# Expert weights of a graph-plus-MoE layer converted as 12 whole chunks through a ring of three, in place of 24 halves through a ring of six

## The reference, cut to what matters

```
x = x + gnn(_layernorm(x), edges, ...)               # two GAT layers, residual products
x = x + ffn(_layernorm(x)[None], ...)[0]
# in ffn, after attention (x is now the sum so far, h2 its layernorm):
gate_logits = h2 @ Wg                                # 625 x 8, top 1, softmax of one = 1
hid = relu(einsum('nd,edf->enf', h2, W1) + b1)       # W1: 8 x 768 x 3072
y   = einsum('enf,efd->end', hid, W2) + b2           # W2: 8 x 3072 x 768
moe = einsum('ne,end->nd', combine, y)
```

## Time and profile before

| | us |
|---|---|
| median of 3 runs (lowest, highest) | 1209.26 (1204.29, 1209.5) |
| the profiled execution | 1207.77 |
| its span in the profile | 1205.9 |
| TensorE matmul busy | 1054.9 (87%) |
| DVE busy | 762.9 (63%) |
| ACT busy | 557.0 (46%) |
| GpSimd busy | 155.0 (13%) |

### The profile page before, as it was taken

One profiled execution on the slowest core, in us unless ns is written; L12 is line 12 of the kernel. 1 busy time (PEld: TensorE's weight loads), 2 busy tenths in 40 slices (PEclk: granted clock), 3 DMA queues, 4 the chain that ended last, 5 costly groups with the idle time before them and its releaser, 6 DMA issues.

```text
span 1205.9 us, 19078 instructions
## 1 busy us (share of the span) xinstructions
PE 1054.9 (87%) x6178; PEld 659.4 (55%) x6179; DVE 762.9 (63%) x1337; ACT 557.0 (46%) x740; POOL 155.0 (13%) x135
## 2 busy tenths in 40 slices
PE   5989778999789769989989307999999999999997
PEld 3555467646656546556768203555555555555554
DVE  6677678773445763449966419893113999889711
ACT  2676556303131234248843018772113777778511
POOL 3100000280003322126001320000000000000000
PEclk9999889999889879989999658999999999999999
DMA  8920200022401440020000389996001999999501
GB/s 310 366 71 0 105 1 1 1 105 77 79 1 65 79 79 1 1 101 2 2 2 1 81 185 390 357 388 230 13 26 32 372 378 391 367 392 374 193 13 29
DMA packets 98378, 170.63 MB, mean 141 GB/s; under 512 B 38611, under 2 KB 38691, under 8 KB 98330
## 3 DMA queue, kind: packets, MB, share of 16 engines
q1 hardware_dynamic: 88138, 145.33, 35.0%
q0 software_dynamic: 6016, 16.80, 4.4%
q10 hardware_dynamic: 4176, 7.87, 2.0%
HBM read 153.19 MB, written 18.79 MB: 143 GB/s over the span
## 4 chain that ended last, share of the span: by engine, by line
PE 67%; DVE 16%; DMA 5%; issue 5%; ACT 4%; POOL 1%; DVEq 1%; ACTq 0%; SPq 0%; POOLq 0%
PE psum L1309 30%; PE psum L1529 15%; PE psum L1508 14%; DMA low<-in_L_ffn_W_dram 2%; DVE area L1250 2%; PE psum L1346 2%; PE psum L1298 2%; DMA sorted_tokens<-area,smalls 2%; PE psum L1517 2%; DVE smalls L900 1%; ACT area L829 1%; PE psum L1425 1%; DVE low L912 1%; DVE area L1156 1%; DMA low<-sorted_tokens 1%
## 5 line engine op out<-in xcount | busy, mean ns | idle before, releaser
L1309 PE MATMUL psum<-area,low 128*125 128x256 f16 (+2 forms) x1080 | 249.1, 392 | 21.6 <-DVE low L1095 11.2
L1250 DVE TENSOR_TENSOR area<-low,area 128x1536 f16<-128x1536 f32 x144 | 245.5, 1753 | 18.3 <-ACT area L829 18.1
L1529 PE MATMUL psum<-area,low 128*128 128x384 f16 x1296 | 217.9, 326 | 5.6 <-DVE area L1250 4.5
L829 ACT ACTIVATE area<-low 128x1536 f16<-128x1536 f32 x144 | 208.2, 1482 | 28.3 <-DMA low<-in_L_ffn_W_dram 20.9
L1508 PE MATMUL psum<-area,low 128*128 128x512 f16 x972 | 220.7, 381 | 0.0
L1309 PEld LDWEIGHTS psum<-area,low 128*125 128x125 f16 (+1 forms) x1080 | 150.8, 151 | 115.0 <-issue 63.4
L1529 PEld LDWEIGHTS psum<-area,low 128*128 128x128 f16 x1296 | 126.4, 98 | 85.3 <-DVE area L1250 6.8
L1309 PE MATMUL psum<-area 125*128 125x64 f16 (+9 forms) x1076 | 145.2, 287 | 16.3 <-DVE area L1237 8.0
L1508 PEld LDWEIGHTS psum<-area,low 128*128 128x128 f16 x972 | 95.5, 98 | 113.8 <-issue 3.0
L1309 PEld LDWEIGHTS psum<-area 125*128 125x128 f16 (+3 forms) x1076 | 93.8, 127 | 51.3 <-issue 14.4
L840 ACT ACTIVATE low<-psum 128x512 f32<-128x512 f32 x54 | 31.9, 591 | 156.5 <-PE psum L1508 143.7
(11 more groups left out here) (203 smaller groups left out, 1253.0 us busy)
## 6 DMA issues: line engine op xcount, KB each, us to landing
low<-in_L_ffn_W_dram SPq DMA_DIRECT2D x144, 768.0 KB, 8.1
area<-in_L_gnn_W_dram SPq DMA_DIRECT2D x2, 3072.0 KB, 11.6
area<-in_L_gnn_Wr_dram SPq DMA_DIRECT2D x2, 3072.0 KB, 15.7
sorted_tokens<-area POOLq DMA_DIRECT2D x3, 1792.0 KB, 16.5
sorted_totals<-area POOLq DMA_DIRECT2D x3, 1792.0 KB, 28.7
low<-sorted_tokens ACTq DMA_DIRECT2D x11, 384.0 KB, 6.9
low<-sorted_totals ACTq DMA_DIRECT2D x9, 384.0 KB, 3.0
area<-in_L_ffn_Wv_dram SPq DMA_DIRECT2D x6, 384.0 KB, 6.3
```

What stands on the lines that cost most here:

```text
L829: act.activation(unit_parts(u)[0], raw_view(u), ACT.Copy).then_inc(high_ok, 1)
L1250: dve.tensor_tensor(low_, raw_view(u), high_, ALU.subtract).then_inc(low_ok, 1)
L1309: ins = pe.matmul(place(name)[0:parts, at:at + w], left(q), right(q)[:, at:at + w], start=(q == 0), stop=(q == k - 1))
L1529: ins = pe.matmul(psum[:, (4 + q) * BANK:(4 + q) * BANK + D // 2], hidT[c % 2][x_][:, j, :], w2_s[c][w_][:, j, q * D // 2:(q + 1) * D // 2 ...
```

## The change

The unit becomes the whole chunk. There are 12 units in place of 24, the ring has 3 places of 3072 columns in place of 6 of 1536 (the same memory in the same order), each unit is one transfer, one ACT operation and one DVE operation. Since 12 units don't divide evenly over 8 slices, STEPS gives the slices 2, 1, 2, 1, 2, 1, 2, 1 units: in halves 4, 2, 4, 2, ... where 3, 3, 3, 3, ... stood. SP's wait for the scattered totals stays ahead of the third chunk.

```diff
-        RING = 6
-        raw = [low[:, at + q * W1W:at + (q + 1) * W1W] for at in (TW, TW + 2 * XW, TW + XW) for q in range(2)]
+        RING = 3
+        raw = [low[:, at:at + 2 * W1W] for at in (TW, TW + 2 * XW, TW + XW)]
...
-        UNITS = [(w, c, q) for s in range(1, C + 2) for w, c in ((1, s - 1), (2, s - 2)) if 0 <= c < C
-                 for q in range(2)]
+        UNITS = [(w, c) for s in range(1, C + 2) for w, c in ((1, s - 1), (2, s - 2)) if 0 <= c < C]
...
-            w, c, q = UNITS[u]
-            n = (KD if w == 1 else CK) // 2
-            return [part[:, q * n:(q + 1) * n, :] for part in (w1_s if w == 1 else w2_s)[c]]
+            w, c = UNITS[u]
+            return (w1_s if w == 1 else w2_s)[c]
...
-            wait_split(eng, a, unit_of[w, c, 1])
+            wait_split(eng, a, unit_of[w, c])
...
-        AHEAD, PER_STEP = 3, U // (C + 2)
-        assert U % (C + 2) == 0
+        AHEAD = 3
+        STEPS = [(0, 2), (2, 3), (3, 5), (5, 6), (6, 8), (8, 9), (9, 11), (11, 12)]
+        assert U == STEPS[-1][1] and len(STEPS) == C + 2
...
-            for u in range(k * PER_STEP, (k + 1) * PER_STEP):
+            for u in range(*STEPS[k]):
                 convert(a, b, u)
...
-                    for u, (w, c, q) in enumerate(UNITS):
-                        if u == 4:
+                    for u, (w, c) in enumerate(UNITS):
+                        if u == 2:
                             sp.wait_ge(totals_scattered, 16 * T)
...
-                            half_chunk = W1[bass.ds(e, 1), q * D // 2:(q + 1) * D // 2, c * CW:(c + 1) * CW]
+                            chunk = W1[bass.ds(e, 1), :, c * CW:(c + 1) * CW]
                         else:
-                            half_chunk = W2[bass.ds(e, 1), c * CW + q * CW // 2:c * CW + (q + 1) * CW // 2, :]
-                        sp.dma_start(raw_view(u), half_chunk.rearrange("a (k p) n -> p (a k) n", p=128))\
+                            chunk = W2[bass.ds(e, 1), c * CW:(c + 1) * CW, :]
+                        sp.dma_start(raw_view(u), chunk.rearrange("a (k p) n -> p (a k) n", p=128))\
                             .then_inc(raw_in[u % RING], 16)
```

More of the change, by code:

```diff
@@ L228, in unit_parts @@
         def unit_parts(u):
-            w, c, q = UNITS[u]
-            n = (KD if w == 1 else CK) // 2
-            return [part[:, q * n:(q + 1) * n, :] for part in (w1_s if w == 1 else w2_s)[c]]
+            w, c = UNITS[u]
+            return (w1_s if w == 1 else w2_s)[c]
         def raw_view(u):
-            return v3(raw[u % RING], (KD if UNITS[u][0] == 1 else CK) // 2)
+            return v3(raw[u % RING], KD if UNITS[u][0] == 1 else CK)
         smalls = ctx.enter_context(nc.sbuf_tensor("smalls", [128, 528], F32))
```

## The result

The changed kernel takes 1249.14 us (median of 4 runs, 1245.64 to 1253.91), the kernel before 1206.92 beside it (1204.29 to 1209.5): ratio 1.035, 95% interval 1.031 to 1.040. That is slower by 42 us; the forecast was 1232, with 1220 to 1243 as its range. The direction held and so did the kind of wait, the size did not.

The account below looks back on a forecast made before the run. TensorE was taken to set the time, with DVE and DMA right behind. Five times (2.7 + 2.05) less 3.7 us of old waits, plus 3.4 at the start, gave 23.5 us more: 1232 us, range 1220 to 1243.

Parts of the forecast that it names:

- Operations: Whole-chunk conversions take about 3.35 us on DVE, 2.76 on ACT; 5 us saved on DVE, worth nothing by itself.
- Term 1: At each of five changes of expert, a fourth half on DVE ahead of the last hidden chunk: TensorE waits 2.7 us.
- Term 2: Ring of three wholes turns slower: 2.05 us more wait before a new expert's first second product, five times.
- ten waits or so: Sign: TensorE's idle time ahead of second products grows from 5.6 to 25 us or more, released by DVE.
- Later steps of the block have slack: In a new expert's block, later conversions are early enough: DVE ends hidden chunk 2 near 1024.2, TensorE wants it at 1026.8.
- The landing of 7.0: A 1536 KB transfer into the ring takes 7.0 us from issue to landing, range 6.4 to 8.3.
- Term 3: First expert: transfers pace ACT's ten halves before the first relu; first second product starts 3.4 us later (2.8 to 4.7).
- Rival (b): Clock falls to 1.2 GHz ahead of first expert's first relu: 4 us more, 1236; chance 0.11 together with landing over 8.3.
- (a): Ring keeps up; only the waits at expert changes and 1 us at the start cost, 14.5 us, 1222; chance 0.14.
- (c): Larger transfers relieve the DMA engines in the expert phase, the 3.7 us of waits go: 1203, faster; chance 0.04.
- (d): No change: DVE savings and shorter queues cover all the losses; chance 0.05.
- A DMA share that stays at 1: Sign of being wrong: DMA busy share in streaming stretches not falling below 1, meaning more loss from the slower ring.

Follow-up runs that it names:

- e5: Changed kernel loading only half of each whole's bytes (768 KB), both conversions reading that half twice: 1216.13 us.
- e6: Changed kernel with 40 spare matmuls on TensorE ahead of its wait for the last hidden chunk, in blocks before a new expert: 1249.67 us.
- e8: Kernel before, with half transfers and half conversions, but a chunk's two halves requested only when both places are free: 1215.48 us.
- e3: Changed kernel with each whole loaded by two 768 KB transfers issued together, conversions still whole: 1246.34 us.
- e9: Changed kernel with both loads of a block's token rows (384 KB each) cut to 16 columns: 1246.44 us.
- e4: Changed kernel with slices of 1, 2, 1, 2, ... wholes, so one whole instead of two ahead of the last hidden chunk: 1255.65 us.
- e7: Kernel before with slices of 3, 3, 3, 2, 4, 3, 3, 3 halves, one fewer ahead of a block's first hidden chunk: 1199.95 us, again 1202.4.

## Why the prediction was right or wrong

- *Operations* (3.35 and 2.76 us, each engine less busy): right to 0.01 us, and rightly worth nothing.
- *Term 1* (2.7 us, five times): right where the ring is full, 2.75 in block 3, and in all five changes of e5. Its sentence "transfers can't change it" is one step that failed. It rested on rows of the kernel before, where all halves had landed by then. In the changed kernel units 0 and 1 of the next expert are still on their way (ACT's waits for them at 998.79 and 1002.84), so in the streaming blocks and the first one the stall is 5.3 to 6.0.
- *Term 2* is the other step that failed, and the larger one. The mechanism, the slower turn of the ring, was right, but it was followed through one change of expert only and as a delay on top of a TensorE-bound block. Its wait of 2 us ahead of the first second product of a new expert's block stands in one block of five (2.07 in block 7); in the others it is 0 to 0.55 us, and the loop's delay shows in the stall of term 1. That DVE's low parts were waited for ten times, and "ten waits or so" were forecast, is luck. The check that was missing is one division: a turn was 7.0 + 2.76 + 3.35 = 13.1 us by the prediction's own figures, four are 52.4, already above the 51.3 that TensorE needs. Then every microsecond of landing costs four a block. "Later steps of the block have slack" was drawn from the same single pass.
- *The landing of 7.0*: mis-sized, 8.7 measured in the stream (8.5 over all). 6.4, interpolated for quiet queues, was exact: the least one is 6.4. The high end of 8.3 was too low. With 8.7, 0.2 of hand-overs and 6.3 for the conversions the division gives 15.2 x 4 = 61 us a block, against 59.4 to 60.5 measured, and terms 1 and 2 are inside it, not on top. The size mattered as much as the division: with 7.0 the same division gives 54.0, no more than TensorE's 51.3 and term 1 take together (54.1), and with the high end of 8.3 it gives 59.2.
- *Term 3*: 3.4 us until the first second product, 3.8 measured (749.65 against 745.88). DVE came as forecast, with the hidden part at 749.04 for the forecast 749.2; TensorE didn't wait for it, since it came half a microsecond later still, behind the product at the lower clock. The rest of block 0 lost 7.2 more, where term 1 had 2.7: it streams as well.
- *Rival (b)*, the clock, came true where it was looked for, after a stand of 5.15 us ahead of the first relu, but the slow product was mostly hidden behind the wait for DVE and cost about 0.5 us, not 4. It also fell at four changes of expert, where no term had it; e6 shows that this cost nothing inside the stream and 1.7 us at its end. *Rivals (a), (c), (d)* are out. For (c), rates fell with the larger transfers, from 387 to 330 GB/s, since the requests came late.
- "A DMA share that stays at 1 would mean more loss": it fell to 0.93 as term 2 has it, and the loss was larger all the same.
- *What the Trainium skill says* of breaking up instructions ("Perfetto Trace Analysis", Optimizing Scalar/DVE Operations): the runs agree, e8 is 31 us under e3 with half conversions in place of wholes, part of which can be the order of the slices. Its 1 MiB a transfer ("DMA: Bandwidth & Descriptors", Rules for kernel authors) isn't borne out for a ring of this memory: transfers of 768 KB moved 387 GB/s in it, and of 1536 KB 330.

What stays open: why a landing takes 8.7 us in the stream and 6.4 at the least. e9 leaves token rows a small share. Transfers of neighbouring units on the same engines are the likely rest. The changed kernel's trace points that way, without proving it: over the 59 wholes from the second expert's second on, landing time rises with what the two transfers ahead still had to go at the issue (correlation 0.68). With 7.5 us to go it was 9.65, with 1.5 twice 6.4, but with 2.5 once 10.45. A ring of four wholes wasn't tried.

## What to carry to other kernels

Before units are made larger in a ring of fixed memory, divide: places over the time of one turn (landing, every conversion in full, the next request) must give more units per microsecond than the consumer takes, with the landing time as it is under load. Do it with the range of landing times, since each microsecond counts once a turn. When the loop bounds, all engines look less busy, and neither another order (e4) nor a better clock inside the stream (e6) gave anything back here; smaller units did, at each stage of the loop that can then begin on the first half. And when it doesn't bound, one conversion moved from ahead of a hand-over to behind it was worth 5 to 7 us here (e7), as much as the 5 us of DVE time that larger operations could save at best.

## What the runs showed of the hardware that was not expected

A TensorE that stood for 5.5 us in the middle of steady work had the 1.2 GHz level when it started again (0.50 from 1008 to 1010 us, a product of 6.09 us). After a stand of 2.59 us, runs differ: the product took 4.06 us in the change (block 3) and in three of five such places of e5, but 5.47 and 5.50 us in the two others, and 5.74 in e9's block 3. So one trace that keeps the clock doesn't show that such a stand is safe. A transfer of 1536 KB took 6.4 us at the least and 8.7 us on the mean among its like, at only 330 GB/s; the 6.4 that was interpolated from transfers on quiet queues wasn't its latency under load.
